# One-hots of the expert lookup made by one-operand VectorE instructions, with the gate multiplied in, and GpSimd out of the last stage

## The chip, the cores and the metric

The kernel runs on one core of a Trainium2 chip. The metric is device time of one launch in microseconds (us), the median of repeated runs. The engines are named as the profile names them: PE is TensorE's matmuls and PEld its weight loads, DVE is VectorE, ACT is ScalarE, POOL is GpSimd, SP is SyncE.

## The reference

One decoder layer on `x` of 32 × 256 tokens with 256 channels, all in fp32: attention without softmax, an alignment step (dynamic time warping) against a context, and a feed-forward part that picks experts by product keys. The change touches the feed-forward part alone:

```python
q = (xn @ w_q.T).reshape(b, s, 2, NH, KD).transpose(2, 0, 1, 3, 4)
sim = jnp.einsum('pbnhd,hkpd->pbnhk', q, keys_p)          # 2 x 8 heads x 64 keys
scores, idx = jax.lax.top_k(sim, K)                       # K = 8
all_scores = (scores[0][..., :, None] + scores[1][..., None, :]).reshape(b, s, NH, K * K)
all_idx = (idx[0][..., :, None] * NK + idx[1][..., None, :]).reshape(b, s, NH, K * K)
sc, pk = jax.lax.top_k(all_scores, K)
indices = jnp.take_along_axis(all_idx, pk, axis=-1)
wd = down[indices]
hmid = jnp.einsum('bnd,bnhkd->bnhk', inputs, wd)
hmid = jax.nn.sigmoid(sc) * jax.nn.gelu(hmid, approximate=False)
wu = up[indices]
return jnp.einsum('bnhk,bnhkd->bnd', hmid, wu)
```

Each token has 8 heads × 8 experts = 64 picks. Only the first 4096 experts can be picked (64 × 64 index pairs).

## The kernel before

The kernel has three stages, one after another; the last, the expert stage, begins near 568 us of the profiled execution. There is no scheduler: each engine has its own instruction list, written out by hand, and semaphores between them.

The expert stage works on 32 groups (`GROUPS`) of 256 tokens. It does not gather rows. For each group it computes the hidden value of all 4096 experts densely (`hidden`, PE, L1002; gelu by ACT in `gelu`, L1104, into `gelh`), then multiplies it by a coefficient that is the sum of the gates of the picks which name that expert and zero elsewhere, and multiplies by the up table (`output`, PE, L1025). The coefficients come from one-hots. A pick's expert number is split in two parts, and for each token PE multiplies two one-hot matrices with the picks on the partitions (`coefs` on PE, L1015): `hot_hi`, 128 wide, and `hot_lo`, 64 wide, which carries the gate. The product lands in PSUM (`ps_a`) and DVE multiplies it into `gelh` (`coefs` on DVE, L1220).

The picks of the group's two tiles stand together: `valsT[:, par, v, n]` holds on its 128 partitions the 64 picks of token n of the first tile and the 64 picks of token n of the second, a token pair, with v = 0 for the high part, 1 for the low part, 2 for the gate. The 128 pairs of a group are worked in `NQ` = 16 steps of `TQ` = 8 pairs. In step q:

- DVE, `hots`: compares `iota` with the high part for the 8 pairs (L1207, 128 × 1024) and `offs` with the low part (L1209, 128 × 512), both as one instruction with a broadcast second operand.
- POOL, `gated`: multiplies `hot_lo` in place by the gate (L954, 128 × 512), then signals `gated_ready`.
- PE: waits for `gated_ready` of step q and for `coef_ready` of step q - 2 (two PSUM banks), then 32 small matmuls (L1015), then 8 matmuls of `hidden` for the next group (L1002).
- DVE, `coefs`: waits for these matmuls (`a_mm`), then L1220.

`hot_hi` and `hot_lo` have `BUFS` = 4 buffers, and DVE's list runs 3 steps ahead (`AHEAD`): in step q it makes the one-hots of step q + 3, then does the `coefs` of step q; the last three steps make the next group's first three one-hots. Behind the one-hots of q = 3, 4, ... it stands in this order: `norm` of the group before after `coefs` of step 0, `scale` of it after step 6 (L1237, L1242). After step 15 comes `route` twice (L1153 to L1196), the top-k of the group after next. On PE, after step 15: the first `score` (L982), a quarter of `output` (32 matmuls), the second `score`, and the other three quarters (96 matmuls). `output` waits for `coef_ready` of all 16 steps. Groups 2 to 29 stand in a hardware loop of two groups a turn; groups 0, 1, 30 and 31 are written out. Groups 30 and 31 have no `route`, and group 31 no `hidden`.

Of the kernel before, what the change touches and what calls it, by code (L numbers as in the profile page):

```python
# [15 lines left out]
ALU = mybir.AluOpType  # L16
# [3 lines left out]
P = 128  # L20
# [5 lines left out]
def decoder_layer(nc, x, xT, ctx_rows_d, ctx_cols_d, wqkvT_d, bqkv_d, projT_d, projb_d, gamma_d, beta_d, wq_d,  # L26
# [19 lines left out]
    with ctx:  # L46
        def sb(name, shape, dt=F32):
            return ctx.enter_context(nc.sbuf_tensor(name, shape, dt))

        def sem(name):  # L50
            return ctx.enter_context(nc.semaphore(name))
# [12 lines left out]
        iota = sb("iota", [P, T])  # L64
# [81 lines left out]
        pool_rests, dve_rests, act_rests = sem("pool_rests"), sem("dve_rests"), sem("act_rests")  # L146
# [15 lines left out]
        gate_ready = sem("gate_ready")  # L162
        valsT_mm = sem("valsT_mm")
        valsT_ready = sem("valsT_ready")
        hot_ready = sem("hot_ready")
        gated_ready = sem("gated_ready")
        a_mm = sem("a_mm")
        coef_ready = sem("coef_ready")
# [13 lines left out]
        def rest(eng, spare):  # L182

            eng.sem_inc(spare, 1)

        def later(b, n):

            return not (isinstance(b, int) and b < n)

        def pipeline(eng, stages, peel, unroll=2, total=NB):  # L190

            def step(i, par):
                for stage, lag in stages:
                    if lag is None:
                        stage()
                        continue
                    b = i - lag
                    if not isinstance(b, int) or 0 <= b < total:  # L200
                        stage(b, (par + lag) % 2)
            for i in range(peel):
                step(i, i % 2)
            with eng.Fori(0, (total - peel) // unroll) as j:
                for u in range(unroll):
                    step(j * unroll + (peel + u), (peel + u) % 2)
            for i in range(total, total + max(lag or 0 for _, lag in stages)):
                step(i, i % 2)
# [8 lines left out]
        with ExitStack() as st:  # L217
# [33 lines left out]
            block = st.enter_context(nc.Block())  # L251
# [4 lines left out]
            @block.sync  # L256
            def _(sp):
                def one(ap, b):
                    return ap[bass.ds(b, 1)].rearrange("a p t c -> (a p) t c")

                def load_xT(b, par):
                    if isinstance(b, int) and b == 1:
                        for dst, src in ((projT[:, :], projT_d), (proj[HS:HS + 1, :], projb_d),
                                         (gamma[:, :], gamma_d), (beta[:, :], beta_d)):
                            sp.dma_start(dst, src).then_inc(p_in, 16)
                    if isinstance(b, int) and 2 <= b < 2 + NB // 8:
                        some = slice(8 * (b - 2), 8 * (b - 1))
                        sp.dma_start(ctx_rows[:, some, :], ctx_rows_d[some].rearrange("b s c -> s b c"))\
                            .then_inc(ctx_in[b - 2], 16)
                        sp.dma_start(ctx_cols[:, :, some, :],  # L270
                                     ctx_cols_d[:, some].rearrange("(k p) b s -> p k b s", k=CC))\
                            .then_inc(ctx_in[b - 2], 16)
                    if later(b, 2):
                        sp.wait_ge(qkv_mm, b - 1)
                    sp.dma_start(xT_sb[:, par], one(xTb, b)).then_inc(xT_in[par], 16)

                def load_x(b, par):
                    if later(b, 2):
                        sp.wait_ge(sum_done, b - 1)
                    sp.dma_start(x_sb[:, par], one(xb, b)).then_inc(x_in[par], 16)  # L280

                def store_x1(b, par):
                    sp.wait_ge(x1_ready, b + 1)
                    sp.dma_start(one(x1b, b), x1_sb[:, par]).then_inc(x1_out[par], 16)

                def store_dist(b, par):
                    sp.wait_ge(root_ready, b + 1)
                    sp.dma_start(dist_d[bass.ds(b, 1)].rearrange("a (i j) -> (a i) j", i=RP),
                                 dist_sb[:, par]).then_inc(dist_out[par], 16)

                for part in range(3):
                    of = slice(HS * part, HS * (part + 1))
                    at = slice(GAP * part, GAP * part + HS)
                    sp.dma_start(wqkv[:, :, at], wqkvT_d[:, of].rearrange("(k p) d -> p k d", k=CC)).then_inc(w_in, 16)
                    sp.dma_start(bias[at, :], bqkv_d[of]).then_inc(w_in, 16)

                pipeline(sp, [(load_xT, 0), (load_x, 5), (store_x1, 7), (store_dist, 10)], 12)
                for par in range(2):
                    sp.wait_ge(x1_out[par], 16 * NB // 2)
                    sp.wait_ge(dist_out[par], 16 * NB // 2)  # L300
# [246 lines left out]
        with ExitStack() as st:  # L547
# [32 lines left out]
            block = st.enter_context(nc.Block())  # L580
# [267 lines left out]
        with ExitStack() as st:  # L848
            def se(name, shape, dt=F32):
                return st.enter_context(nc.sbuf_tensor(name, shape, dt))  # L850
# [3 lines left out]
            NQ = 16  # L854
            TQ = P // NQ
            CL = 32
            BUFS = 4
# [3 lines left out]
            hot_hi = se("hot_hi", [P, BUFS, TQ, P])  # L861
            hot_lo = se("hot_lo", [P, BUFS, TQ, 2 * CL])
            offs = se("offs", [P, 2 * CL])
# [13 lines left out]
            valsT = se("valsT", [P, 2, 3, P])  # L877
# [18 lines left out]
            def groups(eng, step):  # L896

                for g in range(2):
                    step(g, g)
                with eng.Fori(1, GROUPS // 2 - 1) as j:  # L900
                    for par in range(2):
                        step(2 * j + par, par)
                for g in range(GROUPS - 2, GROUPS):
                    step(g, g % 2)
# [5 lines left out]
            block = st.enter_context(nc.Block())  # L910
# [34 lines left out]
                for par in range(2):  # L945
                    sp.wait_ge(y_out[par], 16 * GROUPS // 2)

            @block.gpsimd
            def _(pool):
                def gated(g, par, q):  # L950

                    pool.wait_ge(hot_ready, g * NQ + (q + 1))
                    rest(pool, pool_rests)
                    pool.tensor_tensor(hot_lo[:, q % BUFS], hot_lo[:, q % BUFS],  # L954
                                       valsT[:, par, 2, TQ * q:TQ * (q + 1), None].to_broadcast([P, TQ, 2 * CL]),
                                       ALU.mult).then_inc(gated_ready, 1)

                def step(g, par):
                    for q in range(NQ):
                        gated(g, par, q)  # L960
                groups(pool, step)

            @block.tensor
            def _(pe):
                def turn(g, par):
# [180 lines left out]
            def _(dve):  # L1146
# [52 lines left out]
                def hots(g, par, q):  # L1199

                    if q == 0:
                        dve.wait_ge(valsT_ready, g + 1)
                    if later(g, 1) or q >= BUFS:
                        dve.wait_ge(a_mm, g * NQ + (q + 1 - BUFS))
                    rest(dve, dve_rests)
                    some = slice(TQ * q, TQ * (q + 1))
                    dve.tensor_tensor(hot_hi[:, q % BUFS], iota[:, None, 0:P].to_broadcast([P, TQ, P]),  # L1207
                                      valsT[:, par, 0, some, None].to_broadcast([P, TQ, P]), ALU.is_equal)
                    dve.tensor_tensor(hot_lo[:, q % BUFS], offs[:, None, :].to_broadcast([P, TQ, 2 * CL]),  # L1209
                                      valsT[:, par, 1, some, None].to_broadcast([P, TQ, 2 * CL]), ALU.is_equal)\  # L1210
                        .then_inc(hot_ready, 1)

                def coefs(g, par, q):

# [37 lines left out]
                for q in range(AHEAD):  # L1252
                    hots(0, 0, q)
# [3 lines left out]
                def step(g, par):  # L1257
                    for q in range(NQ):
                        if q + AHEAD < NQ:
                            hots(g, par, q + AHEAD)  # L1260
                        elif within(g, 1):
                            hots(g + 1, 1 - par, q + AHEAD - NQ)
                        coefs(g, par, q)
                        if q == 0 and later(g, 1):
                            norm(g - 1, 1 - par)
                        if q == 6 and later(g, 1):
                            scale(g - 1, 1 - par)
                    if within(g, 2):
                        route(g + 2, 0)
                        route(g + 2, 1)  # L1270
# [46 lines left out]
```

## Time and profile before

| | |
|---|---|
| median of 3 runs | 3309.46 us (3308.94 to 3311.43) |
| profiled execution, its own time | 3312.22 us |
| span of the profile | 3310.5 us |
| mean granted TensorE clock | 0.935 of full speed |
| PE, PEld, DVE, ACT, POOL busy | 91%, 72%, 84%, 22%, 18% |

Busy shares are means over three stages with different limits. Where a row gives the start of two instructions that follow each other on an engine, the difference of the starts is what the first one costs the engine; the duration of one instruction is longer, since its end overlaps the next one's beginning. The profiled execution took 2.8 us more than the median.

### The profile page before, as it was taken

Reading aid. Unit: us, or ns where it says so; the run is one execution under the profiler, and the core shown is the slowest. Engines: PE = TensorE matmul, PEld = TensorE weight load, DVE = VectorE, ACT = ScalarE, POOL = GpSimd, SP = SyncE. Lnnn points to the kernel's source line nnn. Section 1 sums busy time; section 2 is a strip of 40 time slices with the busy share of each in tenths; the row PEclk is TensorE's granted clock in tenths of the full one; section 3 lists DMA queues with packets and bytes.
Section 4 is the critical chain, followed back from the end, with each engine's and each line's share of the span. In section 5 each row is a group of like instructions: output and inputs, shape, how many; then the busy total and the mean of one; then the engine's idle time right before and its main releaser. Section 6 shows DMA issues by size and latency. Waiting matters only on the chain.

```text
span 3310.5 us, 73159 instructions
## 1 busy us (share of the span) xinstructions
PE 3016.2 (91%) x26660; PEld 2388.6 (72%) x26660; DVE 2774.3 (84%) x8246; ACT 736.2 (22%) x1302; POOL 597.7 (18%) x599
## 2 busy tenths in 40 slices
PE   8981047699999999999999999999999999999997
PEld 4651035588888888888888888888888888888886
DVE  5557977798889898989898988888888888888865
ACT  3540024212222222222222222222222222222210
POOL 1230000022222121212122222222222222222221
PEclk9985555899999999999999999999999999999997
DMA  5441025200000000000000000000000000000000
GB/s 154 140 132 46 0 73 172 73 1 11 11 11 11 11 11 11 11 11 11 11 11 11 11 11 11 11 12 11 12 11 12 11 11 11 11 11 11 8 8 7
DMA packets 88552, 93.42 MB, mean 28 GB/s; under 512 B 6109, under 2 KB 86910, under 8 KB 88062
## 3 DMA queue, kind: packets, MB, share of 16 engines
q1 hardware_dynamic: 88206, 88.74, 8.6%
q8 instruction: 225, 3.69, 0.4%
q14 instruction: 121, 0.99, 0.1%
HBM read 60.94 MB, written 27.79 MB: 27 GB/s over the span
## 4 chain that ended last, share of the span: by engine, by line
PE 80%; DVE 2%; issue 0%; ACT 0%; DVEq 0%; ACTq 0%
PE bank L1002 29%; PE bank L1025 27%; PE bank L1015 16%; PE bank L982 7%; PE bank L973 1%; DVE hot_hi L1207 1%; PE bank L992 0%; ACT dnT L1117 0%; DVE top_i L1157 0%; DVE gelh L1220 0%; DVE hot_lo L1209 0%; DVE top L1153 0%; DVE sel_i L1171 0%; DVE sel L1167 0%; DVEq L1238 0%
## 5 line engine op out<-in xcount | busy, mean ns | idle before, releaser
L1002 PE MATMUL bank<-x2T,dnT 128*128 128x256 f32 x4096 | 1011.8, 390 | 0.4 <-ACT gelh L1104 0.4
L954 POOL TENSOR_TENSOR hot_lo<-hot_lo,valsT 128x512 f32<-128x512 f32 x512 | 536.1, 1047 | 2492.5 <-DVE hot_lo L1209 2492.5
L1207 DVE TENSOR_TENSOR hot_hi<-iota,valsT 128x1024 f32<-128x1024 f32 x512 | 858.7, 1677 | 52.2 <-issue 36.7
L1025 PE MATMUL bank<-up,gelh 128*128 128x256 f32 x4096 | 896.6, 380 | 0.9 <-DVE gelh L1220 0.9
L1025 PEld LDWEIGHTS bank<-up,gelh 128*128 128x128 f32 x4096 | 779.8, 190 | 133.1 <-issue 28.7
L1002 PEld LDWEIGHTS bank<-x2T,dnT 128*128 128x128 f32 x4096 | 738.1, 190 | 111.2 <-issue 1.3
L1015 PEld LDWEIGHTS bank<-hot_lo,hot_hi 128*64 128x64 f32 x16384 | 529.5, 140 | 195.7 <-issue 178.5
L1015 PE MATMUL bank<-hot_lo,hot_hi 128*64 128x64 f32 x16384 | 600.2, 227 | 28.2 <-DVE gelh L1220 27.6
L1104 ACT ACTIVATE gelh<-bank 128x512 f32<-128x512 f32 x512 | 305.7, 597 | 938.6 <-PE bank L1002 937.9
L1220 DVE TENSOR_TENSOR gelh<-bank,gelh 128x512 f32<-128x512 f32 x512 | 347.6, 679 | 52.4 <-PE bank L1015 49.6
L1209 DVE TENSOR_TENSOR hot_lo<-offs,valsT 128x512 f32<-128x512 f32 x512 | 349.5, 683 | 0.0
L1153 DVE MAX8 top<-bank 128x8 f32<-128x64 f32 x1024 | 140.8, 216 | 145.0 <-PE bank L982 144.8
L982 PE MATMUL bank<-keymap,xnT 128*128 128x512 f32 x512 | 237.6, 608 | 9.5 <-DVE top_i L1157 6.2
L1157 DVE FIND_INDEX8 top_i<-top,bank 128x8 uint32<-128x64 f32 x1024 | 205.1, 225 | 0.0
L982 PEld LDWEIGHTS bank<-keymap,xnT 128*128 128x128 f32 x512 | 99.6, 195 | 110.6 <-issue 103.2
L1104 ACT ACT_TABLE_LOAD x62 | 79.5, 1283 | 382.1 <-PE bank L1002 382.1
L677 PE MATMUL bank<-fold,lo_hi 128*80 128x32 f32 x4 | 0.7, 326 | 178.0 <-DVEq L780 178.0
L677 PEld LDWEIGHTS bank<-fold,lo_hi 128*80 128x80 f32 x4 | 0.6, 242 | 178.2 <-DVEq L780 178.2
L1093 ACT ACTIVATE vals<-sel 128x64 f32<-128x64 f32 x64 | 16.5, 257 | 413.0 <-DVE sel L1167 412.7
L1093 ACT ACT_TABLE_LOAD x32 | 41.1, 1283 | 298.6 <-DVE sel L1167 298.6
L1171 DVE FIND_INDEX8 sel_i<-sel,pair 128x8 uint32<-128x64 f32 x512 | 101.1, 220 | 0.0
L1179 DVE TENSOR_TENSOR pick<-half_i,iota 128x512 f32<-128x512 uint32 x128 | 82.8, 689 | 4.8
(140 smaller groups left out, 1994.2 us busy)
## 6 DMA issues: line engine op xcount, KB each, us to landing
x_scratch<-x_sb SPq DMA_DIRECT2D x64, 256.0 KB, 2.2
xT_sb<-in_xT SPq DMA_DIRECT2D x32, 256.0 KB, 2.7
x_sb<-in_x SPq DMA_DIRECT2D x32, 256.0 KB, 2.8
x_again<-x_scratch SPq DMA_DIRECT2D x32, 256.0 KB, 2.6
x_tile<-x_scratch SPq DMA_DIRECT2D x32, 256.0 KB, 3.0
x_res<-x_scratch SPq DMA_DIRECT2D x32, 256.0 KB, 2.8
out_y<-yo SPq DMA_DIRECT2D x32, 256.0 KB, 2.2
gelh<-in_table SPq DMA_DIRECT2D x4, 1024.0 KB, 8.9
```

The source lines that it names most:

```text
L954: pool.tensor_tensor(hot_lo[:, q % BUFS], hot_lo[:, q % BUFS], valsT[:, par, 2, TQ * q:TQ * (q + 1), None].to_broadcast([P, TQ, 2 * CL]), ...
L982: mm = pe.matmul(ps_score[p][:, :], xnT[:, k, a, :], keymap[:, k, p * NH * NK:(p + 1) * NH * NK], start=(k == 0), stop=(k == CC - 1))
L1002: mm = pe.matmul(ps_h[q % 2][:, c, :], dnT[:, k, 2 * q + c, :], x2T[:, k, :, :].rearrange("p a t -> p (a t)"), start=(k == 0), stop=(k == ...
L1015: mm = pe.matmul(ps_a[q % 2][rows, t * 2 * CL:(t + 1) * 2 * CL], hot_hi[:, q % BUFS, t, rows], hot_lo[:, q % BUFS, t, :], start=True, stop ...
L1025: mm = pe.matmul(ps_out[:, a, :], gelh[:, par, c, a, :], up[:, c, :], start=(c == 0), stop=(c == CL - 1))
L1104: act.activation(gelh[:, par, 2 * q:2 * q + 2, :, :].rearrange("p c a t -> p c (a t)"), ps_h[q % 2], ACT.Gelu).then_inc(gel_ready, 1)
L1153: dve.max(out=top[:, p, h, :], in_=ps_score[p][:, h * NK:(h + 1) * NK])
L1157: last = dve.max_index(out=top_i[:, p, h, :], in_max=top[:, p, h, :], in_values=ps_score[p][:, h * NK:(h + 1) * NK])
L1171: dve.max_index(out=sel_i[:, h, :], in_max=sel[:, h, :], in_values=pair[:, h, :, :].rearrange("p a b -> p (a b)"))
L1207: dve.tensor_tensor(hot_hi[:, q % BUFS], iota[:, None, 0:P].to_broadcast([P, TQ, P]), valsT[:, par, 0, some, None].to_broadcast([P, TQ, P] ...
L1209: dve.tensor_tensor(hot_lo[:, q % BUFS], offs[:, None, :].to_broadcast([P, TQ, 2 * CL]), valsT[:, par, 1, some, None].to_broadcast([P, TQ, ...
L1220: dve.tensor_tensor(some, ps_a[q % 2][:, :].rearrange("p (t a c) -> p c a t", t=TQ, a=2), some, ALU.mult)\
```

## The change

The two broadcast comparisons of a step become 16 instructions, two for each pair: one compares `iota[:, 0:128]` with one `[P, 1]` column of `valsT`, and one compares `offs` with the low part's column and multiplies by the gate's column in the same instruction. The pool block of this stage, its multiplications and `hot_ready` go; DVE signals `gated_ready` itself after the last of the 16. The values computed are the same.

```diff
-        hot_ready = sem("hot_ready")
...
-            @block.gpsimd
-            def _(pool):
-                def gated(g, par, q):
-
-                    pool.wait_ge(hot_ready, g * NQ + (q + 1))
-                    rest(pool, pool_rests)
-                    pool.tensor_tensor(hot_lo[:, q % BUFS], hot_lo[:, q % BUFS],
-                                       valsT[:, par, 2, TQ * q:TQ * (q + 1), None].to_broadcast([P, TQ, 2 * CL]),
-                                       ALU.mult).then_inc(gated_ready, 1)
-
-                def step(g, par):
-                    for q in range(NQ):
-                        gated(g, par, q)
-                groups(pool, step)
-
...
-                    some = slice(TQ * q, TQ * (q + 1))
-                    dve.tensor_tensor(hot_hi[:, q % BUFS], iota[:, None, 0:P].to_broadcast([P, TQ, P]),
-                                      valsT[:, par, 0, some, None].to_broadcast([P, TQ, P]), ALU.is_equal)
-                    dve.tensor_tensor(hot_lo[:, q % BUFS], offs[:, None, :].to_broadcast([P, TQ, 2 * CL]),
-                                      valsT[:, par, 1, some, None].to_broadcast([P, TQ, 2 * CL]), ALU.is_equal)\
-                        .then_inc(hot_ready, 1)
+                    for t in range(TQ):
+                        at = TQ * q + t
+                        dve.tensor_scalar(hot_hi[:, q % BUFS, t, :], iota[:, 0:P], valsT[:, par, 0, at:at + 1], None,
+                                          ALU.is_equal)
+                        last = dve.tensor_scalar(hot_lo[:, q % BUFS, t, :], offs[:, :], valsT[:, par, 1, at:at + 1],
+                                                 valsT[:, par, 2, at:at + 1], ALU.is_equal, ALU.mult)
+                    last.then_inc(gated_ready, 1)
```

VectorE's list at the head of the hardware loop, from the end of the second `route` (line 1196) to step 0's `coefs` (line 1220) and `norm`, before:

```order
L1196 SCALAR_TENSOR_TENSOR vals<-upper,half_key 128x64
L1207 TENSOR_TENSOR hot_hi<-iota,valsT 128x1024 [waits a_mm]
L1209 TENSOR_TENSOR hot_lo<-offs,valsT 128x512
L1220 TENSOR_TENSOR gelh<-bank5,gelh 128x64x8 [waits gel_ready,a_mm]
L1226 TENSOR_TENSOR y3<-bank7,x2_res 128x512 [waits res_in0,out_mm]
```

Two VectorE instructions stand between the routing and the first `coefs` there.

VectorE's list of the changed kernel in the same step, here of group 0, where `norm` does not stand (lines 1180, 1192, 1194 and 1205 are the places of 1196, 1207, 1209 and 1220 before; the pair of lines 1192 and 1194 stands eight times in a row, the six in the middle are left out):

```order
L1180 SCALAR_TENSOR_TENSOR vals<-upper,half_key 128x64
L1192 TENSOR_SCALAR hot_hi<-iota,valsT 128x128
L1194 TENSOR_SCALAR hot_lo<-offs,valsT 128x64
...
L1205 TENSOR_TENSOR gelh<-bank5,gelh 128x64x8 [waits gel_ready,a_mm]
L1192 TENSOR_SCALAR hot_hi<-iota,valsT 128x128 [waits a_mm]
```

Sixteen instructions stand where two stood; the waits are at the same places, and nothing else on VectorE has moved.

TensorE's list in a step before, the small matmuls (line 1015) and the next group's `hidden` (line 1002):

```order
L1015 MATMUL bank6<-hot_lo,hot_hi 64x64 [waits coef_ready,gated_ready]
L1015 MATMUL bank6<-hot_lo,hot_hi 64x64 x15
L1002 MATMUL bank4<-x2T,dnT 128x256 [waits gel_ready,x2T_ready]
L1002 MATMUL bank4<-x2T,dnT 128x256 x3
```

TensorE's list in the same step of the changed kernel:

```order
L999 MATMUL bank6<-hot_lo,hot_hi 64x64 [waits coef_ready,gated_ready]
L999 MATMUL bank6<-hot_lo,hot_hi 64x64 x15
L986 MATMUL bank4<-x2T,dnT 128x256 [waits gel_ready,x2T_ready]
L986 MATMUL bank4<-x2T,dnT 128x256 x3
```

TensorE's instructions and waits are the same; only the engine that signals `gated_ready` is another.

## Rows read from the trace of the kernel before

**Rows 1.** The page: busy time by engine

```profile
PE 3016.2 (91%) x26660; PEld 2388.6 (72%) x26660; DVE 2774.3 (84%) x8246; ACT 736.2 (22%) x1302; POOL 597.7 (18%) x599
```

**Rows 2.** Windows: busy time of each engine, granted TensorE clock (PEclk), DMA share

```profile
500.00:540.00 40.00, 33.65 (x97) 22.86 (x97) 34.12 (x121) 21.40 (x48) 0.00 (x0) 0.50 0.49 157
...
1000.00:1500.00 500.00, 500.00 (x4749) 403.91 (x4749) 448.07 (x1345) 104.36 (x162) 100.33 (x97) 1.00 0.04 11
```

**Rows 3.** Timeline of PE over one group: start us, us, instruction

```profile
1488.76 1.15 PE L1015 MATMUL bank<-hot_lo,hot_hi 128*64 128x64 f32 x32
...
1491.76 1.15 PE L1015 MATMUL bank<-hot_lo,hot_hi 128*64 128x64 f32 x32
...
1540.86 7.07 PE L1025 MATMUL bank<-up,gelh 128*128 128x256 f32 x32
...
1572.02 1.15 PE L1015 MATMUL bank<-hot_lo,hot_hi 128*64 128x64 f32 x32
```

**Rows 4.** Timeline of DVE in the same group: [idle before <-releaser]

```profile
1501.39 0.68 DVE L1220 TENSOR_TENSOR gelh<-bank,gelh 128x512 f32<-128x512 f32 x1
1501.99 1.77 DVE L1207 TENSOR_TENSOR hot_hi<-iota,valsT 128x1024 f32<-128x1024 f32 x1
...
1504.29 0.68 DVE L1220 TENSOR_TENSOR gelh<-bank,gelh 128x512 f32<-128x512 f32 x1
...
1510.70 0.15 DVE L1237 RECIPROCAL rs<-sd 128x2 f32<-128x2 f32 x1
1510.93 0.94 DVE L1242 TENSOR_SCALAR yo<-y,mv,rs 128x256 f32<-128x256 f32 x2
1511.80 1.21 DVE L1207 TENSOR_TENSOR hot_hi<-iota,valsT 128x1024 f32<-128x1024 f32 x1
...
1541.17 2.20 DVE L1153 MAX8 top<-bank 128x8 f32<-128x64 f32 x16 [3.73 <-PE bank L982]
...
1570.24 1.22 DVE L1207 TENSOR_TENSOR hot_hi<-iota,valsT 128x1024 f32<-128x1024 f32 x1
...
1573.33 0.69 DVE L1220 TENSOR_TENSOR gelh<-bank,gelh 128x512 f32<-128x512 f32 x1 [1.27 <-PE bank L1015]
...
1575.71 1.23 DVE L1207 TENSOR_TENSOR hot_hi<-iota,valsT 128x1024 f32<-128x1024 f32 x1
```

**Rows 5.** Timeline of POOL in the same group

```profile
1501.64 1.04 POOL L954 TENSOR_TENSOR hot_lo<-hot_lo,valsT 128x512 f32<-128x512 f32 x1 [1.86 <-DVE hot_lo L1209]
```

**Rows 6.** Waits of DVE, 700 to 3150 us: us in total, times, longest

```profile
DVE top L1153 <- PE bank L982: 135.7, 30, 5.0
DVE hot_hi L1207 <- issue: 36.7, 13, 3.0
```

**Rows 7.** Timeline of DVE, stages 1 and 2: instructions with [P, 1] operands

```profile
67.45 0.40 DVE L516 TENSOR_SCALAR x_sb<-y,mv,rs 128x256 f32<-128x256 f32 x1
...
67.45 0.72 DVE L516 TENSOR_SCALAR x_sb<-y,mv,rs 128x256 f32<-128x256 f32 x2
...
502.98 0.48 DVE L789 SCALAR_TENSOR_TENSOR mask<-iota,bounds,ramp 77x256 f32<-77x256 f32 x1 [0.32 <-issue]
503.38 0.15 DVE L814 SCALAR_TENSOR_TENSOR nb<-mv,rs 128x2 f32<-128x2 f32 x1
```

**Rows 8.** Timeline of DVE in `route`: tensor_scalar with immediates

```profile
1550.45 0.20 DVE L1175 TENSOR_SCALAR half_i<-sel_i 128x64 uint32<-128x64 uint32 x1
1550.56 0.19 DVE L1176 TENSOR_SCALAR half_i<-sel_i 128x64 uint32<-128x64 uint32 x1
```

**Rows 9.** Timelines of DVE and POOL: one tensor_scalar beside a POOL instruction

```profile
61.71 1.10 DVE L516 TENSOR_SCALAR x_sb<-y,mv,rs 128x256 f32<-128x256 f32 x1
...
61.59 1.07 POOL L325 TENSOR_TENSOR x1sq<-x1T 128x512 f32<-128x512 f32 x1 [6.45 <-ACT x1T L434]
```

**Rows 10.** Timeline of PE: group 30, its first step and its `output`

```profile
3154.81 1.15 PE L1015 MATMUL bank<-hot_lo,hot_hi 128*64 128x64 f32 x32
...
3203.09 27.79 PE L1025 MATMUL bank<-up,gelh 128*128 128x256 f32 x128
```

## The prediction

> **What bounds the kernel now.** I read the page first: PE is busy for 91% of the span, DVE for 84% [rows 1]. Such shares are means, so the windows come next. In the expert stage, which is the change's, PE is busy for 500.00 of 500 us at the full granted clock, and DVE for 448 [rows 2]. The bound there is PE, but DVE is only a tenth behind it, and the change works on DVE.
>
> How much room DVE has is read from the timelines of one group. PE starts group after group 1572.02 - 1488.76 = 83.26 us apart, and a step of it (small matmuls and `hidden`) takes 1491.76 - 1488.76 = 3.00 us [rows 3]. On DVE a full step takes 1504.29 - 1501.39 = 2.90 us: 0.60 for `coefs` (1501.39 to 1501.99) and 2.30 for the two one-hots [rows 4]. So in the steps both engines run nearly at one rate. DVE's idle time in a group is 3.73 us before `route`, where it waits for `score`, and 1.27 us before the first `coefs` [rows 4]; behind the jump of the loop it waits up to 3.0 us more, 36.7 us in 13 turns, so 2.8 us in each turn of two groups, or 1.4 us a group [rows 6]. That is 6.4 us a group in all, or 0.40 us for each of the 16 steps. If the new one-hots take more than about 2.30 + 0.40 = 2.7 us a step, DVE cannot keep up. The true limit is a little lower, 2.5 us, because a few of today's one-hots are cheaper than 2.30 and what POOL costs `scale` goes too (both below).
>
> **What the change removes.** POOL's multiplication of 1.04 us a step [rows 5] is not waited for by PE in the loop, since DVE is three steps ahead. But it costs DVE time: `hot_hi` takes 1.77 us beside it and 1.22 us where no POOL instruction runs (the rows at 1501.99 and 1570.24) [rows 4]. Without POOL the old instructions would cost 2.30 - 0.55 = 1.75 us a step; in `scale` the two instructions of L1242 take 0.94 us [rows 4], against 0.72 for the same form without POOL [rows 7], so 0.2 us of the 1.10 from 1510.70 to 1511.80 go. With PE as the bound none of this is worth anything; it sets how much more DVE can bear.
>
> **What it adds.** A step now has 8 instructions of 128 elements with one `[P, 1]` operand (call each A) and 8 of 64 elements with two (B). Neither stands in the trace, so they are put together from neighbours, by start-to-start time.
> - Element and fixed cost. `hot_hi` with 1024 elements and `hot_lo`-sized instructions with 512 take 1.22 and 0.68 us, so 1.05 ns an element; the 0.60 us from 1501.39 to 1501.99 for 512 leaves 0.06 us that each instruction costs whatever its size [rows 4].
> - B. The two `tensor_scalar` of L516 have two `[P, 1]` operands and 256 elements. One takes 0.40 us, both 0.72, so the second starts 0.32 us after the first [rows 7]. At 1.05 ns an element 256 elements would leave 0.32 - 0.27 = 0.05 for everything else, less than the plain fixed cost; at half that rate per element they leave 0.32 - 0.13 = 0.19, which is 0.06 fixed and 0.13 for two operands. The durations allow both: a `tensor_scalar` of 64 elements with immediates lasts 0.19 to 0.20 us [rows 8] against L516's 0.40, and the 192 elements between them make 0.20 at the full rate with the operands free, or 0.10 at half of it with 0.10 left for two operands. I take the second reading for two reasons. The one clean case of a single such operand shows a price: after a 256-element `scalar_tensor_tensor` with one the next instruction starts 503.38 - 502.98 = 0.40 us later, where 0.06 + 0.27 = 0.33 are explained [rows 7], so 0.07 for the operand. And an L516 beside a POOL instruction took 1.10 us instead of 0.40, until POOL's was nearly done [rows 9], as `hot_hi` with its two SBUF inputs is held up, though L516 has one tensor input. So B = 0.32 - 192 × 0.525 ns = 0.22 us.
> - A = 0.06 + 128 × 0.525 ns + 0.065 = 0.19 us.
>
> A rule of the Trainium skill bears on the same choice. "VectorE: DVE Perf Modes", section "The perf-mode tier table", has fp32 `tensor_scalar` at 2× and `tensor_tensor` at 1×, and "SBUF — State Buffer", section "Who interferes with whom", says that a 2-port mode takes the port pair that it shares with GpSimd for the whole instruction; the held-up L516 agrees. With it the sum is the one below; without it, at the full rate, it is the fourth rival.
>
> A step's one-hots: 8 × (0.19 + 0.22) = 3.29 us (with A at 0.191), against 2.30 today. Bounds: B is nearly measured. A could have its operand free, 0.13 us (X = 2.8), or pay as much as two, 0.25 us (X = 3.8). I take the middle, because both rows of [rows 7] give 0.065 to 0.07 for each operand.
>
> **The sum.** DVE's turn for one group, from the start of one `route` to the next: 1570.24 - 1541.17 = 29.07 us to the first one-hots; X for them; 1575.71 - 1573.33 = 2.38 for `coefs` of step 0 and `norm`; 15 steps of X + 0.60; 0.9 for `scale` [rows 4]; 1.4 for the jump of the loop [rows 6]. That is 42.75 + 16 X = 95.4 us with X = 3.29. Nothing hides the jump any more, since DVE is now late everywhere.
>
> Does PE's order add waiting to it? `output` needs `coefs` of step 15. From there PE needs 1572.02 - 1540.86 = 31.16 us for `output` and the second `score`, and some 1.1 us for the small matmuls of step 0, 32.3 us in all [rows 3]; DVE needs 29.07 + 3.29 = 32.4 us until it asks for them. They meet, so the turn stays at 95.4, with PE idle about 0.9 us in each step of 3.89 us.
>
> - 30 groups with `route`: 30 × (95.4 - 83.26) = 364 us.
> - Group 30: its steps took 3203.09 - 3154.81 = 48.3 us [rows 10]. Now 1.1 + 0.6 + 1.8 + 0.9 + 15 × 3.89 = 62.8, so 14.5 more.
> - Group 31: VectorE set its pace already, the 12 one-hots made in it cost some 1.08 us more each, 13 us.
> - Group 0: three one-hots before any PE work, 3 × (3.29 - 1.75) = 5 us.
>
> Together 397 us on the profiled execution's 3312.2, so 3709; the median of the runs lies 2.8 lower, so 3706 us. One step's cost counts some 510 times: 0.1 us on X is 51 us.
>
> **The rivals.** Within 0.2% (6.6 us) is what a measurement of this kernel cannot tell from no change.
> 1. PE's clock falls. With a wait in each step PE would be busy 3.0 of 3.89 us. From 500 to 540 us it was busy for 33.65 of 40 and had 0.50 of the clock, 1.2 of 2.4 GHz [rows 2]. Against it: at half clock a step needs some 6 us of PE, which then is never idle, and a PE without idle time has 1.00 from 1000 to 1500 us [rows 2]; and within the steps PE may lag DVE by a few us before DVE waits. What would show is `output` starting at half clock: 1.7 to 3.4 us for each of 30 groups, 51 to 102 us more, so 3757 to 3808.
> 2. The operand costs A less than taken (A = 0.13 to 0.16): X = 2.8 to 3.05, so 3456 to 3584.
> 3. It is dearer, as much as B's two (A = 0.225 to 0.25): X = 3.56 to 3.8, so 3844 to 3966.
> 4. Full rate per element, free operands: A = 0.32 - 128 × 1.05 ns = 0.185, B = 0.32 - 192 × 1.05 ns = 0.12, X = 2.44. That is just inside DVE's room, so only the ends of the stage pay, some 4 us: 3313, no change. The point from which it decides is X = 2.5.
> 5. The other side: half rate and operands loaded beside the instruction before. A = 0.13, B = 0.06 + 0.03 = 0.09, X = 1.8. PE stays the bound; gained are only group 31, where PE waits for DVE, 12 × 0.45 = 5 us: 3304, at the very edge of faster. The 0.32 us of L516 speaks against it. The Trainium skill, "VectorE: DVE Perf Modes", section "The TRN2 errata — SBUF-src ops pay a fixed extra latency per instruction", gives 58 cycles plus half the elements at 0.96 GHz for such an instruction, with no term for operands, so X = 1.77 by an estimate from its figures, and this same result. Its advice there, tiles of 512 elements or more, speaks against the change.
>
> **How the numbers follow.** Chances: forecast 0.70, its own range 3590 to 3770 (A from 0.165 to 0.205); clock 0.12; cheaper 0.05; dearer 0.05; full rate 0.04; free operands 0.04. The range takes in the forecast and the clock case, 3580 to 3810, and leaves out 0.18. Slower by over 0.2%: 0.92, the first three cases. Same: full rate and most of free operands, 0.06. Faster: what is left of it, 0.02.
>
> **What the changed profile would show.** Right: the two new groups on DVE 512 × 8 each, with 0.19 and 0.22 us between starts; in the loop a DVE step of 3.9 us and a group of 95 us; DVE's wait for `score` gone; PE idle in each step, released by DVE; no POOL in the stage; L1242's twin at 0.72 a pair. Wrong: PE still at 100% of the windows (rival 4 or 5), starts that lie closer or farther apart (2, 3), or PEclk under 1.00 between 1000 and 1500 us (1). The prediction is most exposed to A, which no row shows.

## The result, and the profile after

The changed kernel takes 3733.86 us (3732.48 to 3736.51), against 3309.52 for the kernel before in the same session: 1.128 of its time, 95% interval 1.126 to 1.130. The forecast was 3706 us, 28 us less.

The page of the kernel after: busy time by engine, and the shares of the chain that ended last by engine.

```profile
PE 3058.7 (82%) x26660; PEld 2401.7 (64%) x26660; DVE 3349.4 (90%) x15414; ACT 735.7 (20%) x1302; POOL 61.4 (2%) x87
...
DVE 55%; PE 21%; issue 5%; DVEq 3%; ACT 0%; ACTq 0%
```

Against [rows 1], DVE gained 575 us of busy time and 7168 instructions, POOL lost 536 us, and the chain now runs mostly over DVE. The windows (busy us of PE, PEld, DVE, ACT and POOL, then PEclk, DMA share and GB/s) show where:

```profile
1000.00:1500.00 500.00, 438.33 (x4043) 349.61 (x4042) 479.55 (x2338) 89.83 (x141) 0.00 (x0) 1.00 0.03 9
```

In the same stretch PE had 500.00 of 500 us before [rows 2]; now 438, with its clock still at 1.00. The only new work in this stretch is DVE's. DVE's timeline of the kernel after, from the end of the second `route` of a group to the first `coefs`:

```profile
1520.97 0.28 DVE L1192 TENSOR_SCALAR hot_hi<-iota,valsT 128x128 f32<-128x128 f32 x1
1521.17 0.31 DVE L1194 TENSOR_SCALAR hot_lo<-offs,valsT 128x64 f32<-128x64 f32 x1
1521.39 0.28 DVE L1192 TENSOR_SCALAR hot_hi<-iota,valsT 128x128 f32<-128x128 f32 x1
...
1524.10 0.31 DVE L1194 TENSOR_SCALAR hot_lo<-offs,valsT 128x64 f32<-128x64 f32 x1
1524.93 0.69 DVE L1205 TENSOR_TENSOR gelh<-bank,gelh 128x512 f32<-128x512 f32 x1 [0.53 <-PE bank L999]
```

From 1520.97 to the last of the 16 at 1524.10 are 3.13 us, and one more 64-element instruction costs 1521.39 - 1521.17 = 0.22: a step's one-hots take 3.35 us, where they took 2.30 [rows 4]. The instruction with half the elements but two `[P, 1]` operands is the dearer one.

PE's timeline of the kernel after: two steps of a group and its end, then the `output` of an earlier group and of the one ten groups behind it:

```profile
1539.41 1.15 PE L999 MATMUL bank<-hot_lo,hot_hi 128*64 128x64 f32 x32 [0.69 <-DVE gelh L1205]
1540.49 1.99 PE L986 MATMUL bank<-x2T,dnT 128*128 128x256 f32 x8
1543.36 1.15 PE L999 MATMUL bank<-hot_lo,hot_hi 128*64 128x64 f32 x32 [0.87 <-DVE gelh L1205]
...
1583.10 3.60 PE L966 MATMUL bank<-keymap,xnT 128*128 128x512 f32 x8
1587.60 7.17 PE L1009 MATMUL bank<-up,gelh 128*128 128x256 f32 x32 [0.91 <-DVE gelh L1205]
...
1009.02 7.17 PE L1009 MATMUL bank<-up,gelh 128*128 128x256 f32 x32 [0.91 <-DVE gelh L1205]
...
1973.23 7.17 PE L1009 MATMUL bank<-up,gelh 128*128 128x256 f32 x32 [0.91 <-DVE gelh L1205]
```

A step takes 1543.36 - 1539.41 = 3.95 us, which is 3.35 + 0.60; PE stands idle 0.87 us in it, released by DVE's `coefs`. From the first of these `output` rows to the last, ten groups later, a group takes (1973.23 - 1009.02) / 10 = 96.42 us, against 83.26 [rows 3]. `output` waits too, 0.91 us, for the last `coefs`.

The waits of the kernel after, 700 to 3550 us (us in total, times, longest):

```profile
PE bank L999 <- DVE gelh L1205: 315.7, 341, 1.8
...
DVE hot_hi L1192 <- issue: 37.0, 13, 3.1
...
DVE gelh L1205 <- PE bank L999: 7.7, 15, 0.5
```

DVE's 135.7 us of waiting for `score` [rows 6] have gone altogether. What stays is the jump of the loop, 37.0 us, now on an engine that is late everywhere.

### The profile page after: what moved, and what is told of

It reads as the page before. It is cut to its first block, busy times and chain, and to the rows that moved or that the text cites. A ratio compares the mean times of both kernels' runs of the same rounds, so it can differ in the third digit from the quotient of the medians.

```text
span 3731.1 us, 78826 instructions
## 1 busy us (share of the span) xinstructions
PE 3058.7 (82%) x26660; PEld 2401.7 (64%) x26660; DVE 3349.4 (90%) x15414; ACT 735.7 (20%) x1302; POOL 61.4 (2%) x87
## 3 DMA queue, kind: packets, MB, share of 16 engines
HBM read 60.94 MB, written 27.79 MB: 24 GB/s over the span
## 4 chain that ended last, share of the span: by engine, by line
DVE 55%; PE 21%; issue 5%; DVEq 3%; ACT 0%; ACTq 0%
DVE hot_lo L1194 21%; DVE hot_hi L1192 19%; PE bank L1009 16%; DVE gelh L1205 8%; PE bank L999 2%; PE bank L966 2%; DVE top_i L1141 2%; DVE top L1137 1%; PE bank L986 1%; DVE sel_i L1155 1%; DVE sel L1151 1%; DVEq L1212 1%; DVE yo L1227 0%; DVE pick L1168 0%; DVE pick L1163 0%
## 5 line engine op out<-in xcount | busy, mean ns | idle before, releaser
L1194 DVE TENSOR_SCALAR hot_lo<-offs,valsT 128x64 f32<-128x64 f32 x4096 | 1250.2, 305 | 0.0
L1192 DVE TENSOR_SCALAR hot_hi<-iota,valsT 128x128 f32<-128x128 f32 x4096 | 1131.4, 276 | 52.5 <-issue 37.0
L999 PEld LDWEIGHTS bank<-hot_lo,hot_hi 128*64 128x64 f32 x16384 | 541.2, 140 | 558.6 <-DVE hot_lo L1194 510.2
L1168 DVE TENSOR_TENSOR pick<-pick,top_i 128x512 f32<-128x512 f32 x128 | 82.8, 688 | 4.8
```

The costliest lines, as they stand in the source:

```text
L999: mm = pe.matmul(ps_a[q % 2][rows, t * 2 * CL:(t + 1) * 2 * CL], hot_hi[:, q % BUFS, t, rows], hot_lo[:, q % BUFS, t, :], start=True, stop ...
L1192: dve.tensor_scalar(hot_hi[:, q % BUFS, t, :], iota[:, 0:P], valsT[:, par, 0, at:at + 1], None, ALU.is_equal)
L1194: last = dve.tensor_scalar(hot_lo[:, q % BUFS, t, :], offs[:, :], valsT[:, par, 1, at:at + 1], valsT[:, par, 2, at:at + 1], ALU.is_equal, ...
```

## The experiments

Nine kernels were run. In what follows X is the time of a step's one-hots on VectorE, start to start. "The line" is 3734 - 510 × (3.35 - X) us: the measured time of the changed kernel, and the forecast's 510 steps that count in full. An edit is shown against the kernel that it changes least; where GpSimd's block goes or comes back with it, the text says so.

**Is it the number of instructions, or the `[P, 1]` operands?** The first run takes one operand of the changed kernel away and keeps all instructions:

```diff
-                        dve.tensor_scalar(hot_hi[:, q % BUFS, t, :], iota[:, 0:P], valsT[:, par, 0, at:at + 1], None,
+                        dve.tensor_scalar(hot_hi[:, q % BUFS, t, :], iota[:, 0:P], 7.0, None,
                                           ALU.is_equal)
```

> The changed kernel with the high part compared with the immediate 7.0 instead of its [P, 1] column (so the high one-hots are not those of the reference; everything else is done). Theory, the start-to-start time of a small tensor_scalar is about 0.065 us fixed + 0.52 ns an element + 0.06 us for each [P, 1] operand: the 128-element instruction goes from 0.196 to about 0.135 us, a step's one-hots from 3.35 to 2.86 us, and with 510 steps paid in full the time from 3734 to about 3484 us. Rival, the time goes to the number of instructions and the first operand is free: 0.196 stays, and 3734 us.

Measured: 3498.63 us, ratio to the kernel before 1.057 (1.055 to 1.059). DVE's timeline of this kernel, within a step:

```profile
1502.41 0.20 DVE L1192 TENSOR_SCALAR hot_hi<-iota 128x128 f32<-128x128 f32 x1
1502.54 0.30 DVE L1194 TENSOR_SCALAR hot_lo<-offs,valsT 128x64 f32<-128x64 f32 x1
1502.77 0.21 DVE L1192 TENSOR_SCALAR hot_hi<-iota 128x128 f32<-128x128 f32 x1
```

The 128-element instruction now costs 0.13 us until the next starts, 0.06 less than with its operand, and the other is unchanged. 235 us are gone with one operand. The time lies some 14 us above what was expected; the reason is given below, with e6_hi_ts_lo_tt.

The second run takes the other two operands away as well:

```diff
-                        last = dve.tensor_scalar(hot_lo[:, q % BUFS, t, :], offs[:, :], valsT[:, par, 1, at:at + 1],
-                                                 valsT[:, par, 2, at:at + 1], ALU.is_equal, ALU.mult)
+                        last = dve.tensor_scalar(hot_lo[:, q % BUFS, t, :], offs[:, :], 7.0, 0.5, ALU.is_equal, ALU.mult)
```

> As e1_imm_hi, and the low part and the gate are immediates too (7.0 and 0.5), so no [P, 1] operand is left in the one-hots and the coefficients are not the reference's; the count of instructions is that of the changed kernel. Theory of a price for each operand: the 64-element instruction goes from 0.223 to about 0.10 us, a step to 1.9 us, under what VectorE can bear, so TensorE is the bound again: 3305 us. Rival, the count of instructions is what costs: over 3600 us.

Measured: 3304.70 us, ratio 0.998 (0.997 to 1.000), with as many instructions as the changed kernel. DVE's timeline:

```profile
1508.71 0.22 DVE L1192 TENSOR_SCALAR hot_hi<-iota 128x128 f32<-128x128 f32 x1
1508.84 0.18 DVE L1194 TENSOR_SCALAR hot_lo<-offs 128x64 f32<-128x64 f32 x1
1508.94 0.22 DVE L1192 TENSOR_SCALAR hot_hi<-iota 128x128 f32<-128x128 f32 x1
```

0.13 and 0.10 us. So the two operands of the second instruction cost 0.12 us, and the rate is read off too: 64 elements more cost 0.03 us, 0.5 ns each, half of the 1.05 ns of the broadcast comparisons. (The second instruction also has a second operation; the pair of e3_ts_pool_gate below, with one operation and one operand each, differs by the same 0.03 us.) What is left, some 0.07 us, is the fixed cost. The 16 small instructions without their operands cost the kernel nothing; the 24 operands of a step, at 0.06 us each, are what takes VectorE over its room.

**Does the gate belong in the second instruction?** The 16 instructions of the changed kernel stay, but GpSimd's block is back as it was before, with the gate's multiplication in it; on VectorE:

```diff
-                        last = dve.tensor_scalar(hot_lo[:, q % BUFS, t, :], offs[:, :], valsT[:, par, 1, at:at + 1],
-                                                 valsT[:, par, 2, at:at + 1], ALU.is_equal, ALU.mult)
-                    last.then_inc(gated_ready, 1)
+                        last = dve.tensor_scalar(hot_lo[:, q % BUFS, t, :], offs[:, :], valsT[:, par, 1, at:at + 1],
+                                                 None, ALU.is_equal)
+                    last.then_inc(hot_ready, 1)
```

> The 16 one-operand instructions, but without the gate's column in the second; GpSimd multiplies by the gate as before (the output is the reference's). Theory, a tensor_scalar of this kind runs at two elements a cycle through the port pair that GpSimd uses and cannot run beside it: the 64-element instruction costs 0.16 us, 8 x (0.196 + 0.16) = 2.85, and the first tensor_scalar after coefs is held until GpSimd's multiplication ends, some 0.5 us: 3.35 to 3.4 us a step, 3735 to 3760 us, so nothing is gained by leaving the gate with GpSimd. Rival, no such hold: 2.85 us a step and 3479 us.

Measured: 3713.69 us, ratio 1.122 (1.120 to 1.124). DVE's and POOL's timelines of this kernel:

```profile
1524.84 0.68 DVE L1222 TENSOR_TENSOR gelh<-bank,gelh 128x512 f32<-128x512 f32 x1
1525.44 0.79 DVE L1209 TENSOR_SCALAR hot_hi<-iota,valsT 128x128 f32<-128x128 f32 x1
1526.15 0.24 DVE L1211 TENSOR_SCALAR hot_lo<-offs,valsT 128x64 f32<-128x64 f32 x1
1526.32 0.28 DVE L1209 TENSOR_SCALAR hot_hi<-iota,valsT 128x128 f32<-128x128 f32 x1
...
1525.11 1.04 POOL L954 TENSOR_TENSOR hot_lo<-hot_lo,valsT 128x512 f32<-128x512 f32 x1 [5.30 <-DVE hot_lo L1211]
```

The first `tensor_scalar` after `coefs` lasts 0.79 instead of 0.28 us, and the next one starts at 1526.15, where POOL's 1.04 us from 1525.11 end; `coefs`, with one operand in PSUM, was not held (0.68 us, with POOL's start in the middle of it). So the hold is real: without it X would be 2.87 (a step that isn't held) and the time 3489. The time lies 21 us under the 3735 to 3760 that were expected, which had counted the hold in all 16 steps. Three of them have no POOL instruction beside them, after `route`, `norm` and `scale`, so X = 2.87 + 0.51 × 13/16 = 3.28 and the line gives 3698; measured are 16 more. DVE's wait for PE at step 0 explains 7 of them (14.9 us in this trace against 7.7). Another 6 lie in `scale`, which the line leaves out: each of its two `tensor_scalar` lasts 0.51 us in the mean beside POOL and 0.41 in the changed kernel, 0.2 us in each of 32 groups.

**What was GpSimd's multiplication worth to the kernel before?** GpSimd's block is taken out of it, and nothing put in its place; VectorE signals for it:

```diff
                     dve.tensor_tensor(hot_lo[:, q % BUFS], offs[:, None, :].to_broadcast([P, TQ, 2 * CL]),
                                       valsT[:, par, 1, some, None].to_broadcast([P, TQ, 2 * CL]), ALU.is_equal)\
-                        .then_inc(hot_ready, 1)
+                        .then_inc(gated_ready, 1)
```

> The kernel before without GpSimd's multiplication (the gate is left out of the coefficients, so the output is not the reference's). Theory: hot_hi costs 1.13 instead of 1.70 us start to start in every step, but TensorE bounds the loop, so only the ends gain: 3303 to 3306 us. Rival, VectorE's pace or GpSimd's latency mattered in the loop: under 3290 us.

Measured: 3302.75 us, ratio 0.998 (0.997 to 0.999). The windows of this kernel:

```profile
1000.00:1500.00 500.00, 499.86 (x4748) 403.72 (x4748) 407.93 (x1346) 104.31 (x162) 0.00 (x0) 1.00 0.04 11
```

DVE has 40 us less than in [rows 2], PE still all but 0.14 of the 500. With PE full, a VectorE that is faster still could give something at the ends of the stage alone.

**The two halves of the change.** `hot_hi` as one broadcast comparison, `hot_lo` by 8 instructions with the gate in them, no GpSimd (against the changed kernel):

```diff
+                    some = slice(TQ * q, TQ * (q + 1))
+                    dve.tensor_tensor(hot_hi[:, q % BUFS], iota[:, None, 0:P].to_broadcast([P, TQ, P]),
+                                      valsT[:, par, 0, some, None].to_broadcast([P, TQ, P]), ALU.is_equal)
                     for t in range(TQ):
                         at = TQ * q + t
-                        dve.tensor_scalar(hot_hi[:, q % BUFS, t, :], iota[:, 0:P], valsT[:, par, 0, at:at + 1], None,
-                                          ALU.is_equal)
                         last = dve.tensor_scalar(hot_lo[:, q % BUFS, t, :], offs[:, :], valsT[:, par, 1, at:at + 1],
                                                  valsT[:, par, 2, at:at + 1], ALU.is_equal, ALU.mult)
```

> The second half of the change alone: hot_hi as one broadcast comparison (1.13 us without GpSimd), hot_lo by 8 instructions of two [P, 1] operands with the gate, no GpSimd. Theory: 1.13 + 8 x 0.223 = 2.91 us a step, VectorE still the bound: 3734 - 510 x 0.44 = 3510 us. If a step's cost did not count 510 times, the time would lie off this line.

Measured: 3521.81 us, ratio 1.064 (1.062 to 1.065). DVE's timeline:

```profile
1502.64 1.26 DVE L1191 TENSOR_TENSOR hot_hi<-iota,valsT 128x1024 f32<-128x1024 f32 x1
1503.78 1.91 DVE L1195 TENSOR_SCALAR hot_lo<-offs,valsT 128x64 f32<-128x64 f32 x8
1505.56 0.73 DVE L1206 TENSOR_TENSOR gelh<-bank,gelh 128x512 f32<-128x512 f32 x1
```

X = 1505.56 - 1502.64 = 2.92, as expected; the time is 12 us over the expected 3510. The broadcast comparison of 1024 elements costs 1.14 us, the 8 small ones that could stand for it 8 × 0.196 = 1.57: at twice the rate per element, and still dearer.

The other half: `hot_hi` by 8 instructions, `hot_lo` as one comparison, the gate on GpSimd (against the kernel before):

```diff
-                    dve.tensor_tensor(hot_hi[:, q % BUFS], iota[:, None, 0:P].to_broadcast([P, TQ, P]),
-                                      valsT[:, par, 0, some, None].to_broadcast([P, TQ, P]), ALU.is_equal)
+                    for t in range(TQ):
+                        at = TQ * q + t
+                        dve.tensor_scalar(hot_hi[:, q % BUFS, t, :], iota[:, 0:P], valsT[:, par, 0, at:at + 1], None,
+                                          ALU.is_equal)
```

> The first half alone: hot_hi by 8 instructions of one [P, 1] operand, hot_lo as one broadcast comparison, the gate by GpSimd as before. Theory with the port hold: 8 x 0.196 + 0.60 = 2.17 us, and the first tensor_scalar after coefs held some 0.55 us by GpSimd: 2.72 us a step, over the limit of 2.5: about 3413 us. Rival, no hold: 2.17 us a step and no change from the kernel before, 3309 us.

Measured: 3380.24 us, ratio 1.021 (1.019 to 1.023). DVE's timeline, a step without a POOL instruction beside it and one with, and DVE's waits from 700 to 3100 us:

```profile
1511.89 1.66 DVE L1209 TENSOR_SCALAR hot_hi<-iota,valsT 128x128 f32<-128x128 f32 x8
...
1514.66 2.16 DVE L1209 TENSOR_SCALAR hot_hi<-iota,valsT 128x128 f32<-128x128 f32 x8
...
DVE top L1153 <- PE bank L982: 18.6, 29, 0.6
DVE gelh L1222 <- PE bank L1015: 15.7, 14, 1.1
```

The hold is there, 2.16 against 1.66, so "no hold, no change" falls. The expected 3413 had it in all 16 steps again and is 33 us too high. Counted in 13 of 16 steps, X = 8 × 0.196 + 0.60 + 0.50 × 13/16 = 2.57, and the line gives 3336; measured are 44 more. The waits explain 27 of them: DVE waits 34 us for PE, where the changed kernel has 7.7. `scale` beside POOL explains 6, as in e3_ts_pool_gate. Some 11 us of the 44 stay unexplained. With short steps DVE finishes its one-hots for step 0 before PE finishes `output`, and waits for `score` again. The line is straight only as long as DVE is always last, down to about X = 3.2 (29.07 + X against PE's 32.3 us in the forecast's sum), and bends below. The same two waits stand in e1_imm_hi (16 us) and e5_hi_tt_lo_ts (14 us), 6 to 9 us more than the changed kernel's 7.7: about half of what those two runs lie above their expectations.

**GpSimd out of the stage without small instructions.** There is no GpSimd block; VectorE makes `hot_lo`, then `hot_hi`, each with one broadcast comparison, and then does the multiplication with one more broadcast instruction, the only one shown:

```diff
+                    dve.wait_ge(hot_ready, g * NQ + (q + 1))
+                    rest(dve, dve_rests)
+                    dve.tensor_tensor(hot_lo[:, q % BUFS], hot_lo[:, q % BUFS],
+                                      valsT[:, par, 2, some, None].to_broadcast([P, TQ, 2 * CL]),
+                                      ALU.mult).then_inc(gated_ready, 1)
```

> GpSimd out of the stage in another way: the two broadcast comparisons stay (hot_lo first), and VectorE multiplies hot_lo by the gate in a third instruction of 512 elements behind hot_hi. Theory: 0.60 + 1.13 + 0.60 = 2.33 us a step, what the kernel before takes beside GpSimd (2.30): TensorE bounds the loop and the time is that of the kernel before, 3307 to 3313 us. Rival, the wait for hot_lo's own semaphore or VectorE's extra work pushes a step over 2.5 us: 3340 us or more.

Measured: 3317.50 us, ratio 1.002 (1.001 to 1.003), 4 us beyond what was expected. DVE's timeline and the windows:

```profile
1512.81 0.69 DVE L1192 TENSOR_TENSOR hot_lo<-offs,valsT 128x512 f32<-128x512 f32 x1
1513.41 1.22 DVE L1195 TENSOR_TENSOR hot_hi<-iota,valsT 128x1024 f32<-128x1024 f32 x1
1514.55 0.69 DVE L1199 TENSOR_TENSOR hot_lo<-hot_lo,valsT 128x512 f32<-128x512 f32 x1
1515.15 0.69 DVE L1210 TENSOR_TENSOR gelh<-bank,gelh 128x512 f32<-128x512 f32 x1
...
1000.00:1500.00 500.00, 499.16 (x4745) 403.04 (x4744) 458.44 (x1440) 104.33 (x162) 0.00 (x0) 1.00 0.04 11
```

X = 1515.15 - 1512.81 = 2.34 in every step, where the kernel before has 2.30 in 13 of 16 and 1.73 in the three without POOL. PE misses 0.84 us in 500, some 4 us over the loop (3.6 of them are waits for VectorE's `coefs`), so at 2.34 VectorE begins to be felt. Removing GpSimd costs little this way, but brings no gain.

**The jump of the loop.** The changed kernel with four groups a turn:

```diff
-                with eng.Fori(1, GROUPS // 2 - 1) as j:
-                    for par in range(2):
-                        step(2 * j + par, par)
+                with eng.Fori(0, (GROUPS - 4) // 4) as j:
+                    for u in range(4):
+                        step(4 * j + (2 + u), u % 2)
```

> The changed kernel with four groups in a turn of the hardware loop instead of two: 7 turns instead of 14. Theory: VectorE is late everywhere, so its 2.8 us at each jump is paid in full, and 7 jumps fewer give 20 us: 3714 us. Rival, the jump is hidden behind TensorE's output: 3734 us.

Measured: 3717.29 us, ratio 1.122 (1.120 to 1.124), 16.6 us less than the changed kernel. The wait behind the jump, 700 to 3550 us:

```profile
DVE hot_hi L1192 <- issue: 17.0, 6, 3.0
```

It was 37.0 in 13 turns; the 20 us less on DVE give 17 us of time. The jump is paid, as the sum had it.

**A version that could beat both.** With the gate on ScalarE, and no GpSimd block, VectorE is left alone with 1.73 us a step. On ScalarE, three steps ahead and before the gelu of each step:

```diff
+                    for t in range(TQ):
+                        at = TQ * q + t
+                        last = act.activation(hot_lo[:, q % BUFS, t, :], hot_lo[:, q % BUFS, t, :], ACT.Copy,
+                                              scale=valsT[:, par, 2, at:at + 1])
+                    last.then_inc(gated_ready, 1)
```

> GpSimd out of the stage with the gate on ScalarE, which was busy for 22% of the span: the two broadcast comparisons stay on VectorE, and ScalarE multiplies hot_lo by the gate in 8 activations of 64 elements a step, each with one [P, 1] scale, ahead of the gelu of the step (the output is the reference's). Theory: VectorE is not held up, 1.13 + 0.60 = 1.73 us a step as in e4_tt_no_gate, ScalarE has 8 x 0.22 + 0.6 = 2.4 of TensorE's 3.0 us a step, and the time is that of e4_tt_no_gate give or take ScalarE's latency, 3302 to 3308 us, at most 0.2% faster than the kernel before. Rival, ScalarE's small instructions cost 0.3 us or more: over 3.0 us a step, ScalarE becomes the bound and the time goes over 3330 us.

Measured: 3311.64 us against 3310.99 for the kernel before, ratio 1.000 (0.999 to 1.001). The time lies 4 us over the 3302 to 3308 that were expected. ACT's timeline, the windows, and a wait of PE, 700 to 3150 us:

```profile
1196.42 2.02 ACT L1102 ACTIVATE hot_lo<-hot_lo,valsT 128x64 f32<-128x64 f32 x8
1198.77 0.60 ACT L1089 ACTIVATE gelh<-bank 128x512 f32<-128x512 f32 x1 [0.33 <-PE bank L987]
1199.43 2.02 ACT L1102 ACTIVATE hot_lo<-hot_lo,valsT 128x64 f32<-128x64 f32 x8
...
1000.00:1500.00 500.00, 498.61 (x4742) 402.50 (x4741) 406.77 (x1344) 284.28 (x926) 0.00 (x0) 1.00 0.04 11
...
PE bank L987 <- ACT gelh L1089: 5.5, 12, 0.7
```

ScalarE keeps to TensorE's 3.0 us a step (1199.43 - 1196.42), so it isn't the bound, but PE misses 1.4 us in 500. Most of that is a wait that the kernel before doesn't have: 5.5 us over the loop, in which `hidden` waits for ScalarE's gelu. In the traces the last group's `output` starts 36.3 us after its first step, 7 us sooner than in the kernel before, and that step begins 6 us later: the gain at the end is given back in the loop. No version tried that computes the reference's values beats the kernel before. The two that don't, e2_imm_both with constants in place of the columns and e4_tt_no_gate without the gate, are faster by 0.2%, with intervals that just leave out no change.

## Why the prediction was right, point by point

- **The bound, and VectorE's room.** Shown. With X = 1.9 and 1.73 the time is that of the kernel before less 5 to 7 us (e2_imm_both, e4_tt_no_gate), with 2.34 (e7_tt_dve_gate) it is 7 us more, with 2.57 in the mean (e6_hi_ts_lo_tt) it is 70 more: the point where DVE takes over lies between 2.34 and 2.57, as the 2.5 of the forecast does.
- **The price of the new instructions.** The mechanism is shown by e1_imm_hi and e2_imm_both: some 0.07 us fixed, 0.5 ns an element, 0.06 us for each `[P, 1]` operand. The forecast had 0.06 and 0.065 for the first and the last, and no row of A at all; the two errors have opposite signs, and that they nearly cancel in A is luck. The size was a little off, and it is the term that accounts for the miss: A was taken at 0.191 and is 0.196, B at 0.22 and is 0.223, so X is 3.35, not 3.29. By the forecast's own 51 us for each 0.1 us that is 31 us; 3706 + 31 = 3737, measured 3733.9.
- **DVE's turn.** 42.75 + 16 × 3.35 = 96.35 us; measured 96.42. DVE and PE do meet at step 0: DVE waits there 0.5 us in half of the groups.
- **The groups at the ends.** Group 30's steps take 3610.64 - 3546.61 = 64.0 us in PE's timeline after, 15.7 more than before, forecast 14.5. Group 31's take 56.8 us to its `output`, against 43.3 before, 13.5 more, forecast 13.
- **The jump.** Paid, shown by e8_unroll4: 17 of the 20 us.
- **What POOL costs DVE, and that it is worth nothing under PE's bound.** Shown by e4_tt_no_gate; the 0.55 us a step come back on DVE and 7 us in time.
- **Rivals.** The clock stayed at 1.00 in the loop although PE stood idle for 0.87 us of each 3.95: that rival fell there. It came true once, outside the loop. PE waited 4.73 us for the last `coefs` of group 30, had a mean of 0.60 of the clock in the 4 us from 3610, and needed 29.58 us for the `output` that took 27.79 before [rows 10]. The same 29.58 us stand in e1_imm_hi, e3_ts_pool_gate and e6_hi_ts_lo_tt. Group 31's `output` went the other way: it began at 0.50 of the clock before and at 0.99 here, 27.89 us against 30.21, so the two cancel in the time. Cheaper and dearer operands fell by the starts; the full rate per element by the 0.5 ns in e2_imm_both; free operands by e1_imm_hi. e2_imm_both is what that last rival would have been, and came out at 3305 us, where 3304 was worked out for it.
- **Failed expectations** were of three kinds. The 510 steps count in full only near the changed kernel's own X, and the line bends as PE becomes a second bound (e1_imm_hi 14 us, e5_hi_tt_lo_ts 12 us). GpSimd's hold was counted in 16 steps where it falls in 13 (e3_ts_pool_gate 21 us, e6_hi_ts_lo_tt 33 us, both under what was expected, though the bend adds time to the second). And two runs with VectorE inside its room came out 4 us over their ranges, because PE waits a little for VectorE (e7_tt_dve_gate) or for ScalarE (e9_act_gate).

The errata formula that the forecast cited as a rival (the Trainium skill, "VectorE: DVE Perf Modes", section "The TRN2 errata — SBUF-src ops pay a fixed extra latency per instruction") has no term for operands. Its estimate is 0.127 us for the 128-element form and 0.094 for the 64-element one. The traces agree with it within 0.01 us as long as the scalars are immediates (e2_imm_both: 0.13 and 0.10 us), and are 0.06 us above it for each `[P, 1]` operand.

## What to carry to other kernels

Price a small instruction by the starts in the trace, and by its form: the fixed cost, the elements at the rate of its mode, and each `[P, 1]` operand for itself. One broadcast `tensor_tensor` over 8 columns beats 8 `tensor_scalar` with a column each as long as an instruction has fewer than some 230 elements, by an estimate from the rows above (a `tensor_scalar` with one column costs 0.13 us + 0.52 ns × n, a column's share of the broadcast 0.01 us + 1.04 ns × n), although the `tensor_scalar` runs at twice the rate. Sizes near 230 were not run. And when two engines run at nearly one pace, compute the turn of the second one from its own timeline before giving it work: here 6.4 us of idle time in 83 were all that it had, and some 18 were asked of it (1.05 more in 13 steps, 1.62 in the 3 without GpSimd beside them).

## What the runs showed of the hardware that was not expected

- A `[P, 1]` operand costs VectorE's next start 0.06 us, nearly as much as the whole fixed part of an instruction (some 0.07), and its duration 0.06 too: 0.28 against 0.22 us for the 128-element form, 0.31 against 0.18 for the 64-element form with two.
- TensorE's granted clock was 1.00 from 1000 to 1500 us, although it had a pause of 0.87 us in most steps and was busy for 438 of the 500 us. In the stretch before the expert stage it had 0.50 with 33.65 of 40 us busy [rows 2], and in group 31's steps 0.50 with 19.38 of 40 us busy (3650 to 3690 us). What tells them apart was not tried.
- A small ScalarE activation (64 elements, `[P, 1]` scale) costs 0.24 us start to start (8 of them end in 2.02 us, one lasts 0.34): not cheaper than the 0.22 of VectorE's, but on an engine that had the time.
